# A stage of 25 tiles: rounds of five in which the engines take turns, or each engine a fixed number of tiles apart

## What is computed

```python
x_cat = jax.nn.elu(jnp.concatenate([out1, out2], axis=-1))   # out: (sum of weighted rows / sum of weights) + bias
unified = x_cat @ Wu + bu                                     # 3125 x 512 times 512 x 256
return residual + unified
```

## Time and profile before

| what | us |
|---|---|
| median of 3 runs (4240.96 to 4242.70) | 4242.43 |
| the profiled execution | 4242.47 |
| its span in the profile | 4240.6 |
| first step of a tile in the unify stage, start | 1797.62 |
| first step of the next stage, start | 1974.47 |

### The profile page before, as it was taken

One profiled execution on the slowest core, in us unless ns is written; L12 is line 12 of the kernel. 1 busy time (PEld: TensorE's weight loads), 2 busy tenths in 40 slices (PEclk: granted clock), 3 DMA queues, 4 the chain that ended last, 5 costly groups with the idle time before them and its releaser, 6 DMA issues. The chain is left out here.

```text
span 4240.6 us, 63598 instructions
## 1 busy us (share of the span) xinstructions
PE 3481.7 (82%) x15628; PEld 2329.0 (55%) x15629; DVE 2453.7 (58%) x7750; ACT 1046.0 (25%) x2509; POOL 2138.7 (50%) x1892
## 2 busy tenths in 40 slices
PE   6276777887777777645999999999959799999988
PEld 4145555555555555432555555555545567777754
DVE  7756777777777777645212121212155467777768
ACT  0121222222222222112303031313144323333322
POOL 0356888887878878600777771000000056666610
PEclk9987777777777777776999999999969899999999
DMA  9358555655556665581554544232213144444420
GB/s 394 96 134 288 132 141 135 139 136 135 138 132 141 133 136 134 110 182 28 171 175 147 178 148 124 86 114 83 82 35 116 66 107 113 114 113 115 114 63 22
DMA packets 494780, 546.18 MB, mean 129 GB/s; under 512 B 226047, under 2 KB 396509, under 8 KB 493803
## 3 DMA queue, kind: packets, MB, share of 16 engines
q0 software_dynamic: 142864, 256.80, 25.2%
q1 hardware_dynamic: 339118, 268.48, 21.6%
q10 hardware_dynamic: 12749, 20.33, 1.3%
HBM read 474.83 MB, written 111.55 MB: 138 GB/s over the span
## 5 line engine op out<-in xcount | busy, mean ns | idle before, releaser
L1038 PE MATMUL p_out<-rows,hot 128*128 128x266 f32 x2048 | 817.6, 554 | 31.0 <-DVE rows L1160 23.1
L963 POOL DMA_INDIRECT count_dram<-number,place x384 | 650.6, 1694 | 159.0 <-issue 111.8
L1038 PEld LDWEIGHTS p_out<-rows,hot 128*128 128x128 f32 x2048 | 517.1, 272 | 224.3 <-DVE rows L1160 120.4
L955 POOL DMA_INDIRECT rows<-att_dram,idx x512 | 552.1, 1078 | 163.0 <-issue 128.2
L1506 PE MATMUL p_lo<-cbuf,parts 128*128 128x400 f16 x1750 | 582.2, 333 | 0.0
L1507 PE MATMUL p_hi<-cbuf,parts 128*128 128x400 f16 x1750 | 581.8, 332 | 0.0
L2075 POOL DMA_INDIRECT col_rows<-col_dram,m_idx x440 | 416.5, 947 | 281.2 <-ACT m_idx L2145 170.0
L1575 POOL DMA_INDIRECT rec_dram<-records,edge_place x416 | 403.3, 969 | 131.4 <-issue 126.4
L1535 DVE TENSOR_TENSOR node_sum<-p_hi,low_sb 128x400 f32<-128x400 f32 x80 | 45.9, 574 | 650.0 <-ACT low_sb L1526 650.0
L1978 POOL MEMSET attr_w<- 128x512 f32 x1 | 0.5, 526 | 781.9 <-POOLq L364 781.9
L1160 DVE TENSOR_TENSOR rows<-rows 128x512 f32<-128x512 f32 x512 | 349.3, 683 | 0.2 <-ACT rows L929 0.2
(11 more groups left out here) (391 smaller groups left out, 6175.4 us busy)
## 6 DMA issues: line engine op xcount, KB each, us to landing
cbuf<-by_src SPq DMA_DIRECT2D x40, 2500.0 KB
count_dram<-zeros SPq DMA_DIRECT2D x40, 1000.0 KB, 23.3
dl_rep<-dl_dram SPq DMA_DIRECT2D x128, 256.0 KB
by_src<-count_dram POOLq DMA_DIRECT2D x25, 800.0 KB, 49.7
g_rows<-by_src SPq DMA_DIRECT2D x25, 800.0 KB, 4.3
rec_dram<-blank ACTq DMA_DIRECT2D x1, 17600.0 KB
records<-in_edges POOLq DMA_DIRECT2D x32, 520.0 KB, 4.1
key_rep<-key_dram SPq DMA_DIRECT2D x64, 256.0 KB
```

The lines of the kernel that those rows point to most:

```text
L955: nc.gpsimd.indirect_dma_start(rows[r][:, u, :], None, att_dram, bass.IndirectOffsetOnAxis(ap=idx[r][:, u:u + 1].bitcast(U32), axis=0)).th ...
L963: nc.gpsimd.indirect_dma_start(count_dram, bass.IndirectOffsetOnAxis(ap=place[r][:, n, c:c + 1].bitcast(U32), axis=0), number[r][:, 2 * n ...
L1038: m = nc.tensor.matmul(p_out[q][:, side, 0:HALF], hot[k][:, u, :], rows[k][:, u, side * HALF:(side + 1) * HALF], start=(u == 0), stop=(u = ...
```

## The change

The loop of rounds is written out over all tiles, with the tile numbers as constants. On VectorE a pass t does the first four steps of tile t (`positive`), the sum of tile t - 1 (`negative`) and the add of tile t - 4 (`add_product`). On ScalarE a pass does the exponential of tile t and the copy of tile t - 2. On TensorE a pass does the transposes of tile t and the product of tile t - 1. The buffers are the same, in the same number; one wait is new (ScalarE waits for the product of tile t - 7 before it writes over its `valT`). The fold stands after pass 6 in place of after round 0. SyncE's and GpSimd's parts are unchanged.

```diff
-                        with dve.Fori(0, R) as i:
...
-                            for u in range(5):
-                                t = i * 5 + u
...
-                                o.link(nc.vector.tensor_scalar(val[:, u, :], val[:, u, :], 0.0, -1.0, ALU.max, ALU.add))
-                                dve.wait_ge(exp_ready, t + 1)
-                                TT(val[:, u, :], val[:, u, :], neg[:, u, :], ALU.add).then_inc(elu_ready, 1)
-                            for u in range(5):
-                                t = i * 5 + u
-                                dve.wait_ge(uni_ready, t + 1)
...
+                        def positive(t):
+                            u = t % 5
+                            dve.wait_ge(val_turned, t + 1)
...
+                            o.did(TS(val[:, u, :], val[:, u, :], 0.0, -1.0, ALU.max, ALU.add))
+                            return o.n
...
+                        for t in range(NT + 4):
+                            if t < NT:
+                                done[t] = positive(t)
+                            if 1 <= t <= NT:
+                                negative(t - 1, done[t - 1])
+                            if t >= 4:
+                                add_product(t - 4)
...
+                        for t in range(NT + 2):
+                            if t < NT:
+                                act.wait_ge(neg_ready, t + 1)
+                                nc.scalar.activation(neg[:, t % 5, :], neg[:, t % 5, :], ACT.Exp).then_inc(exp_ready, 1)
+                            if t >= 2:
+                                act.wait_ge(val_turned, 5 + t - 1)
+                                if t >= 7:
+                                    act.wait_ge(uni_ready, t - 6)
+                                nc.scalar.copy(valT[:, (t - 2) % 5], p_val[t % 2][:]).then_inc(valT_ready, 1)
...
+                        for t in range(NT + 1):
+                            if t < NT:
                                 pe.wait_ge(elu_ready, t + 1)
...
-                                pe.wait_ge(valT_ready, t + 1)
...
+                            if t >= 1:
+                                pe.wait_ge(valT_ready, t)
+                                if t >= 3:
+                                    pe.wait_ge(x_added, t - 2)
                                 for k in range(4):
...
+                            if t == 6:
+                                pe.wait_ge(fold_in, 48)
```

More of the change, by code:

```diff
@@ new lines, in negative, with add_product @@
+                        def negative(t, positive_done):
+                            u = t % 5
+                            dve.wait_ge(exp_ready, t + 1)
+                            o.need(positive_done)
+                            TT(val[:, u, :], val[:, u, :], neg[:, u, :], ALU.add).then_inc(elu_ready, 1)
+                        def add_product(t):
+                            dve.wait_ge(uni_ready, t + 1)
+                            TT(x_sb[:, t, :], x_sb[:, t, :], p_uni[t % 2][:], ALU.add).then_inc(x_added, 1)
@@ L1336, in _ @@
+                        done = [0] * NT
+                        for t in range(NT + 4):
[5 more added lines that the diff above has]
+                                add_product(t - 4)
                         TS(edge_place[:], place_sum[:], -1.0, None, ALU.add)
@@ L1361, in _ @@
                         pe.nop().then_inc(val_turned, 5)
-                        def round_of(i):
-                            for u in range(5):
-                                t = i * 5 + u
+                        for t in range(NT + 1):
+                            if t < NT:
                                 pe.wait_ge(elu_ready, t + 1)
-                                if u >= 2 or not is_first(i):
+                                if t >= 2:
                                     pe.wait_ge(valT_ready, t - 1)
@@ L1375, in round_of @@
                                 for k in range(4):
-                                    m = nc.tensor.matmul(p_uni[u % 2][:], valT[:, u, k, :], wu[:, k, :], start=(k == 0), stop=(k == 3))
+                                    m = nc.tensor.matmul(p_uni[(t - 1) % 2][:], valT[:, (t - 1) % 5, k, :], wu[:, k, :], start=(k == 0), stop=(k == 3))
                                 m.then_inc(uni_ready, 1)
[L1379 to L1386, removed]
@@ L1387, in _ @@
-                        r.then_inc(fold_ready, 1)
-                        with pe.Fori(1, R) as i:
-                            round_of(i)
+                            if t == 6:
+                                pe.wait_ge(fold_in, 48)
+                                for m in range(2):
+                                    for k in range(2):
+                                        nc.tensor.matmul(p_fold[m][:], w2[:, k, m * P:(m + 1) * P], wi[:, k, 0:2 * D], start=(k == 0), stop=(k == 1))
+                                    for k in range(2):
+                                        r = nc.tensor.matmul(p_fold[2][:, m * D:(m + 1) * D], w2[:, k, m * P:(m + 1) * P], wi[:, k, 2 * D:],
+                                                             start=(k == 0), stop=(k == 1))
+                                r.then_inc(fold_ready, 1)
```

20 lines of the change are left out of this document (6 added, 14 removed).

## The result

| what | before | after |
|---|---|---|
| median of 4 runs each, us | 4242.57 (4240.96 to 4242.89) | 4163.34 (4161.92 to 4176.67) |
| ratio, 95% interval | | 0.9823 (0.9808 to 0.9838) |
| span of the profiled execution | 4240.6 | 4161.4 |
| stage's first step (`den`) to the next stage's first step | 180.81 | 106.49 |

The account below looks back on a forecast made before the run. Engines taking turns were taken to bound the stage, then the transfers: their end 1894.9, plus 2.0 sharing and 3.3 exit, starts the next stage at 1900.2, not 1974.47; 4242.4 - 74.3 = 4168.1 us, range 4162 to 4184.

## What to carry to other kernels

When several engines each have under half of a stretch and its pieces are independent, set each engine a fixed number of pieces apart and add up the busiest engine's own short intervals: that is the new period. Then look at what was hidden behind the old waits, here a stream of transfers with 78 us to spare, because that is the new end; a wait that is moved around it wins nothing unless the transfers themselves move, and they must not land on a copy with small packets that someone waits for. And a value that arrives "just in time" in one profile should be asked for with several us of room.

## What was not expected of the hardware

- A block was not left while transfers that GpSimd had asked for in it were under way, even with GpSimd's wait for them moved out of it (105.62, where VectorE was done at 92.38). It was left with a transfer of SyncE's under way (the barrier passed at 1894.5, packets until 1895.4). With GpSimd last, 4.0 us pass from the last packet's start to the next stage (3.9 with two transfers moved, 3.0 without the written wait), with VectorE last 1.64 to 1.79 from its end, with SyncE last 1.6 from a landing.
- A 12.5 KB copy in 4-byte packets took 15.2 to 17.9 us alone, 26.3 beside two big transfers, 28.3 beside four, and 110.3 beside the whole stream.
- An engine can stand at the asking: SyncE needed 20.8 us to ask for the fold's copy behind those small packets, and 0.37 without them.
- A 1 KB column behind the same stream landed after 27.9 us in one execution, 35.5 in another and 40.4 in a third.
